# Two tables of steps written anew, and PSUM banks counted on from sequence to sequence

## The reference, cut to what matters

```python
def attention(x):                       # 16 heads of 64, window 64
    xn = x / norm(x) * 16 * gamma
    q, k, v = split(xn @ W_qkv)
    out = softmax(mask(q @ k.T / 8)) @ v          # blocks of 64 queries, this block's and the one before's keys
    out = out * sigmoid(xn @ W_gates + b_gates)   # one gate per token and head
    return out @ W_out

def layer(x, wqkv, wo, w1, w2, ...):    # applied twice; 8 heads of 64, window 128
    h = shift_token(x)                  # the second half of the columns comes from the token before
    q, k, v = split(h @ wqkv)
    q, k = rotary(l2norm(q) * qs, l2norm(k) * ks)
    x = x + softmax(mask(8 * q @ k.T)) @ v @ wo
    a, g = split(layernorm(shift_token(x)) @ w1 + b1)
    return x + (a * gelu(g)) @ w2 + b2

xn = layernorm(x)
result = x + attention(xn) + layer(layer(xn))
```

## Time and profile before

| | us |
|---|---|
| median of three runs | 2006.38 |
| lowest and highest | 2005.78, 2007.42 |
| span of the profiled execution | 2005.4 |
| TensorE busy | 1859.6 |
| ScalarE, VectorE, GpSimd busy | 1383.4, 1289.4, 929.1 |
| DMA: 128.91 MB moved, mean | 64 GB/s |

### The profile page before, as it was taken

One profiled execution on the slowest core, in us unless ns is written; L12 is line 12 of the kernel. 1 busy time (PEld: TensorE's weight loads), 2 busy tenths in 40 slices (PEclk: granted clock), 3 DMA queues, 4 the chain that ended last, 5 costly groups with the idle time before them and its releaser, 6 DMA issues.

```text
span 2005.4 us, 47841 instructions
## 1 busy us (share of the span) xinstructions
PE 1859.6 (93%) x17808; PEld 1564.7 (78%) x17808; DVE 1289.4 (64%) x4125; ACT 1383.4 (69%) x3997; POOL 929.1 (46%) x1315
## 2 busy tenths in 40 slices
PE   6999999999999779999999999999999999999998
PEld 5777787777778658788787887887877878878787
DVE  5543544444443367768777777687777777777765
ACT  5886977778677555866757758667576585675764
POOL 2532542344233454626536446265364562654632
PEclk9999999999999889999999999999999999999999
DMA  3321232223123520110111101304112112011110
GB/s 130 111 81 54 89 90 74 87 71 92 55 88 121 190 67 22 46 54 22 43 34 34 54 14 51 119 15 162 45 32 62 33 46 64 24 53 30 36 46 27
DMA packets 127003, 128.91 MB, mean 64 GB/s; under 512 B 28112, under 2 KB 101940, under 8 KB 126772
## 3 DMA queue, kind: packets, MB, share of 16 engines
q1 hardware_dynamic: 123604, 119.56, 19.2%
q10 hardware_dynamic: 3168, 6.29, 0.9%
HBM read 72.84 MB, written 37.25 MB: 55 GB/s over the span
## 4 chain that ended last, share of the span: by engine, by line
PE 25%; DVE 17%; ACT 16%; POOL 5%; issue 3%; DVEq 0%; POOLq 0%; ACTq 0%; SPq 0%
PE f_bank L1410 11%; ACT f_prob L1644 6%; DVE f_u L1798 5%; POOL f_prob L1363 4%; PE f_scores L1562 3%; DVE f_gu L1794 3%; PE f_bank L1547 3%; ACT f_u L1664 3%; PE f_o_bank L1522 2%; PE f_scores L1489 2%; PE f_bank L1500 2%; ACT f_probT L1585 2%; ACT f_probT L1589 1%; POOL f_norm L1339 1%; ACT f_probT L1588 1%
## 5 line engine op out<-in xcount | busy, mean ns | idle before, releaser
L589 POOL TENSOR_SCALAR a_prob<-a_prob,a_row_inv,a_gate 128x128 f32<-128x128 f32 x512 | 226.1, 459 | 407.0 <-DVE a_row_inv L929 407.0
L1363 POOL TENSOR_SCALAR f_prob<-f_prob,f_row_inv 128x192 f32<-128x192 f32 x512 | 233.4, 476 | 325.8 <-DVE f_row_inv L1740 325.8
L1410 PE MATMUL f_bank<-weights,f_actT 128*128 128x512 f32 x1152 | 307.5, 409 | 9.3 <-DVE f_norm L1688 5.2
L1547 PE MATMUL f_bank<-f_hT,f_w 128*128 128x256 f32 x2112 | 275.4, 285 | 12.5 <-DVE f_gu L1794 12.5
L1547 PEld LDWEIGHTS f_bank<-f_hT,f_w 128*128 128x128 f32 x2112 | 261.1, 190 | 20.0 <-DVE f_gu L1794 18.7
L1410 PEld LDWEIGHTS f_bank<-weights,f_actT 128*128 128x128 f32 x1152 | 208.6, 192 | 66.1 <-DVE f_norm L1688 9.9
L1644 ACT ACTIVATE f_prob<-f_scores,f_neg_max 128x192 f32<-128x192 f32 x512 | 208.5, 426 | 21.3 <-DVE f_neg_max L1732 19.7
L1664 ACT ACTIVATE f_u<-f_gu 128x256 fp32r<-128x256 f32 x192 | 80.2, 418 | 185.4 <-DVE f_gu L1794 185.4
L1339 POOL TENSOR_TENSOR f_norm<-f_norm,f_minus_half 128x16 f32<-128x16 f32 x64 | 192.1, 3003 | 22.7 <-DVE f_norm L1692 19.3
L821 ACT ACTIVATE a_prob<-a_scores,a_neg_max 128x128 f32<-128x128 f32 x512 | 179.9, 390 | 27.8 <-DVE a_neg_max L920 26.5
L612 PE MATMUL a_bank<-a_xT,weights 128*128 128x512 f32 x768 | 193.3, 403 | 1.5 <-DVE a_wgate L898 1.5
(11 more groups left out here) (139 smaller groups left out, 4080.7 us busy)
## 6 DMA issues: line engine op xcount, KB each, us to landing
split_weights<-a_hi_lo SPq DMA_DIRECT2D x16, 512.0 KB, 2.8
x_next<-states SPq DMA_DIRECT2D x32, 256.0 KB, 3.3
tables<-scaled_tables SPq DMA_DIRECT2D x16, 512.0 KB, 5.9
f_x<-states SPq DMA_DIRECT2D x16, 512.0 KB, 5.0
split_weights<-a_hi_lo SPq DMA_DIRECT2D x12, 682.0 KB, 4.1
weights<-split_weights ACTq DMA_DIRECT2D x6, 1024.0 KB, 8.7
f_w<-split_weights SPq DMA_DIRECT2D x4, 1280.0 KB, 11.6
f_v_crossed<-f_v SPq DMA_DIRECT2D x40, 128.0 KB, 2.3
```

Of the source, the lines that this page charges most:

```text
L589: last = nc.gpsimd.tensor_scalar(part, part, row_inv[:, a % 2, head, t:t + 1], gate[:, half, t, h:h + 1], ALU.mult, ALU.mult)
L1363: last = nc.gpsimd.tensor_scalar(part, part, row_inv[:, a % 2, head, t:t + 1], 1.0, ALU.mult, ALU.mult)
L1410: last = nc.tensor.matmul(out, lhs(c, a), rhs(c, b), start=(i == 0), stop=(i == len(order) - 1))
L1547: mm = nc.tensor.matmul(out[:, which * PART:(which + 1) * PART], w1[:, wp, c, col:col + P], hT[:, hp, c, columns_of(a // FH)], start=(i == ...
```

## The change

Both tables of steps are written anew, with the same steps in each. Of the first one a row reads, before and after:

```diff
-A_ORDER = [("load_x", 0), ("scores", 0), ("softmax", 0), ("weights_in", 0), ("scores", 1), ("softmax", 1), ("weigh", 0), ("weights_hi", 0),
+A_ORDER = [("scores", 0), ("scores", 1), ("load_x", 0), ("tables_in", 0), ("softmax", 0), ("softmax", 1), ("project_v", 0),
```

And the banks are numbered through the whole stage: a fill's bank is its number since the start of the stage modulo 3, and it waits for the fill three before it, be that in the pass before. All that named `bank[n % 3]` names `bank_of(it, n)` now, in both stages:

```diff
-def fill_steps(steps, sizes):
+def fills_of(programs, sizes):
-    return [(step, i) for step in steps if step[0] in sizes for i in range(sizes[step[0]])]
+    return [(it, step, i) for it, steps in programs for step in steps if step[0] in sizes for i in range(sizes[step[0]])]
...
-        fills_before, fills_in, fills_last = fill_steps(before, fills), fill_steps(steps, fills), fill_steps(last, fills)
+        all_fills = fills_of([(None, before)] + [(it, steps) for it in range(BATCH - 1)] + [(BATCH - 1, last)], fills)
+        def bank_of(it, n):
+            return bank[(filled.upto(it, n) - 1) % 3]
-        def vacated(it, n):
-            step, i = (fills_before if it is None else fills_last if is_last(it, BATCH) else fills_in)[n]
+        def vacated(fill):
+            it, step, i = all_fills[fill]
...
             def take_bank(it, n):
-                if n >= 3:
-                    pe.wait_ge(*vacated(it, n - 3))
-                elif it is not None:
-                    pe.wait_ge(emptied.sem, emptied.upto(it, -1))
-                    pe.wait_ge(copied.sem, copied.upto(it, -1))
-                return bank[n % 3]
+                fill = filled.upto(it, n) - 1
+                if fill >= 3:
+                    pe.wait_ge(*vacated(fill - 3))
+                return bank_of(it, n)
```

More of the change, by code:

```diff
@@ L791, in gates @@
                     act.wait_ge(bias_negated, 1)
-                nc.scalar.activation(gate_exp[:], bank[n % 3][0:A_HEADS, :], ACT.Exp, bias=bgate[:], scale=-1.0).then_inc(copied.sem, 1)
+                nc.scalar.activation(gate_exp[:], bank_of(it, n)[0:A_HEADS, :], ACT.Exp, bias=bgate[:], scale=-1.0).then_inc(copied.sem, 1)
             for kind, a in before:
@@ L1075, in layers_phase, with bank_of, vacated @@
         copied = count("copied", wholes, credit=1)
-        fills_before, fills_in, fills_last = fill_steps(before, fills), fill_steps(steps, fills), fill_steps(last, fills)
-        def vacated(it, n):
-            step, i = (fills_before if it is None else fills_last if is_last(it, SEQUENCES) else fills_in)[n]
+        all_fills = fills_of([(None, before)] + [(it, steps) for it in range(SEQUENCES - 1)] + [(SEQUENCES - 1, last)], fills)
+        def bank_of(it, n):
+            return bank[(filled.upto(it, n) - 1) % 3]
+        def vacated(fill):
+            it, step, i = all_fills[fill]
             taken = copied if step[0] in wholes else emptied
@@ L1608, in take_raw @@
                     act.wait_ge(filled.sem, filled.upto(it, first + which))
-                    nc.scalar.activation(qk_tok[:, a % TILES, which, :], bank[(first + which) % 3][:], ACT.Copy)
+                    nc.scalar.activation(qk_tok[:, a % TILES, which, :], bank_of(it, first + which)[:], ACT.Copy)
                     if ("project_qk", a - 1) in emptied.firsts(it):
@@ L1614, in take_raw @@
                         act.wait_ge(emptied.sem, emptied.upto(it, -1))
-                    nc.scalar.activation(square[:, which, :], bank[(first + which) % 3][:], ACT.Square).then_inc(raw_taken.sem, 1)
+                    nc.scalar.activation(square[:, which, :], bank_of(it, first + which)[:], ACT.Square).then_inc(raw_taken.sem, 1)
             for kind, a in before:
@@ L1793, in iteration @@
                         place = PART if j == FH - 1 else 0
-                        nc.vector.scalar_tensor_tensor(out=gu[0:m, a % 2, :], in0=bank[n % 3][0:m, place:place + PART], scalar=b1_cols[0:m, 0, j:j + 1],
+                        nc.vector.scalar_tensor_tensor(out=gu[0:m, a % 2, :], in0=bank_of(it, n)[0:m, place:place + PART], scalar=b1_cols[0:m, 0, j:j + 1],
                                                        in1=gu[0:m, a % 2, :], op0=ALU.add, op1=ALU.mult).then_inc(emptied.sem, 1)
```

111 lines of the change are left out of this document (56 added, 55 removed).

## The result

The changed kernel takes 1963.6 us (1962.2 to 1964.2, 4 runs) beside 2006.9 for the kernel before: 0.978 of it, 95% interval 0.977 to 0.980. That is 43 us faster where I forecast 11, and outside the range of 1982 to 2012.

What follows compares the result with a forecast made beforehand. TensorE's work plus its holes, 145.8 us in all, was taken to bound the kernel. First stage -14, passage +9.5, second stage -7, late projection loads +0.5 gave -11, so 1995.5 us; range 1982 to 2012.

Steps and rivals of the forecast that it cites:

- The passage, +9.5: Between the stages: SyncE's later store of the row constants delays TensorE's second stage by 9.5 us, bounds +5 and +15.
- The other estimate of the prediction: Passage between the stages: with 2 us for each of two landings, the loss is +5 us instead of +9.5.
- The banks, 0: Start of a first-stage pass: counting the banks on gives nothing by itself, since two score steps cover the wait.
- First stage, -3.7 a pass: First stage: filled TensorE holes save 3.7 us in three passes and 2.7 in the last, 14 us together.
- My bound of 24 for the first stage: First stage: upper bound of the gain, 24 us, with all holes shown gone, 6.0 a pass.
- Second stage, -0.45 a half: Second stage: holes in transposes 4 and 7 close, 0.45 us a half, 7 us over sixteen; bounds 21 gained, 10 lost.
- Rope 3 behind transpose_h 1 pushes VectorE's chain: Second stage, up steps: the later rope 3 pushes VectorE's chain by some 0.6 us, so no gain of 0.78 counted.
- rival 3: Second stage: later rope 3 and bias on GpSimd block VectorE's up products, 0.6 us a half slower, 2012.5 us; 20%.
- The other meeting that the prediction names: First stage: rms_apply's products no longer meet GpSimd's table scaling, saving VectorE about two microseconds that TensorE did not await.
- Filled holes come back at the ups: Second stage: each filled hole returns at the up steps, as the chain of VectorE and ScalarE has no slack.
- Rival 1: Only the first stage gains; holes filled in the second come back at the up steps: 2002.5 us; 22%.
- Rival 2: Nearly all holes close, up steps included, and the passage costs only its lower bound: 1980 us; 13%.

Runs made afterwards that it cites:

- a4: The changed kernel with weights_out 6, rows_in and rows_out put back to SyncE's places before the change: 1948.3 us, ratio 0.971; run again 1950.3, 0.973.
- c4: The changed kernel with only rows_in and rows_out put back early, weights_out 6 still ahead of the first rows: 1956.7 us, ratio 0.974 to the kernel before.
- a3: The kernel before with both old tables, only the banks counted on as in the change: 2005.8 us, ratio 1.000.
- b1: The kernel before with project_qk 16 between transposes 14 and 15 and weights_hi, lo and out 6 late: 1997.2 us, ratio 0.996.
- c3: The kernel before with rope 3 and, right behind it, x1_bias moved behind transpose_h 1: 2004.7 us, ratio 0.999.
- b3: The kernel before with rope 3 alone moved behind transpose_h 1, x1_bias left where it was: 2029.6 us, ratio 1.013.
- b2: The kernel before with down 3 moved behind up 4 and down 4 behind up 7: 2005.7 us, ratio 1.001.
- d1: The kernel of a4 with transpose 1 behind scores 3 and down 7 ahead of transpose_qk 2: 1946.6 us, ratio 0.971 to the kernel before.
- c2: The kernel before with the second stage's order from up 0 to the end of a half as in the change: 1998.0 us, ratio 0.995.
- a2: The kernel before with the change's second-stage table and banks, the first stage's table old: 1977.1 us, ratio 0.985.
- a1: The kernel before with the change's first-stage table and banks, the second stage's table old: 1988.0 us, ratio 0.991.
- c1: The kernel before with transpose_qk 0 and take_o 1 behind values 3, rope 2 behind take_o 3: 1999.7 us, ratio 0.996.

## Why the prediction was wrong

The sign was right, and so were most of the places; the sum was not. Of the 32 us by which it fell short, some 11 are in the first stage (20 in the three full passes and 5 in the last, against 13.8), 2 in the passage (7.4 instead of 9.5), some 16 in the second stage (23.1 in fifteen halves and 0.6 in the last, less 0.7 ahead of them, against 6.8), and 3.4 are the clock of the kernel before in its last pass. Point by point:

- *The passage, +9.5.* The chain was right (shown by a4), and the bounds +5 and +15 held; the hole grew by 7.4. From the issue of weights_out 6 to TensorE's start the prediction has 15.5 us (677.5 to 693.0) and the profile 13.5 (649.37 to 662.91): the ten issues took 0.6 more than forecast, the constants 3.8 us from the end of the last load's issue (655.84) to their store instead of 2.5, and from the store's issue to TensorE it was 3.2 instead of 7.2, since the store landed in 2.6 us instead of 6. That the last pass with the passage lost 8.9, so near to 9.5, is luck: it holds the 1.3 of the wait at transpose 1. The other estimate of the prediction, 2 us for each landing and so +5, was off by about as much the other way.
- *SyncE's order inside the first stage, no term.* The late rows_in and rows_out make SyncE late for keep_keys at the start of the next pass, and that cost 0.8 to 1.3 us in each pass but the first (after against a4 and c4).
- *The banks, 0.* Right: a3.
- *First stage, -3.7 a pass.* The mechanism was right and the size wrong. Between profiles of the old table and the new one (a3 and a4, the mean of three passes) a pass lost 7.1 us of waits, start to start. The single terms: transpose 0, 0.51 (forecast 0.55); values 4, 0.96 (0.87); project_out 1, 0.60 (0.43); transpose 6, 0.48 (0.31); values 10, 0.55 (0.48); transpose 5, +0.37 (+0.5). All near. But some 0.5 of the 7.1 is the clock, which fell in two of a3's three passes and in one of a4's: where it stayed full, a pass takes 163.1 and 156.4, 6.7 less. And transposes 14 and 15 gave 2.6 (forecast 0.6 + 0.98), where b1, the moves that I had named, gives 2.05, and what gives the rest is not run; transposes 2 and 3 gave 0.5 where I counted nothing; and some ten waits of 0.1 to 0.3 us that leave no idle row (transposes 8 and 9, scores 11, project_out 10, project_v 7 among them) gave some 0.7 us.
- *The step that failed: a hole costs what its idle row says, and where there is no idle row there is no delay.* I added up idle rows. The window of the third pass shows 3.9 us less idle and 5.8 us less time, and over the kernel 16.7 us went out of TensorE's busy time. My bound of 24 for the first stage, "all holes shown", was thus no bound: the three full passes gave 20 (493.1 to 473.0), and the last one 6.3 without the late stores (154.9 in a3, 148.6 in a4), 26 together.
- *Second stage, -0.45 a half.* Mis-sized by the most. In the medians, a half is 2.1 us shorter in a4 than in a3: 1.4 in the middle of the half (forecast 0.56 + 0.1), 0.7 in the ups and downs (forecast 0, less 0.2 for the late transpose_qk 3), and at the start 0.1 is lost (forecast 0). Of the middle, project_qk 3 gave 0.37 instead of 0.1, and transposes 4 and 7 0.40 and 0.48 instead of 0.22 and 0.34.
- *Rope 3 behind transpose_h 1 pushes VectorE's chain.* Wrong: c3 shows no loss. What the text of rival 3 feared, GpSimd's bias beside VectorE, is real, but it needs the bias at another place (b3). The other meeting that the prediction names went as it said: the products of rms_apply, 32 in all, took 22.4 us before and 13.3 after, 2.3 less a pass.

```profile
L883 DVE SCALAR_TENSOR_TENSOR x_next<-a_x_tok,a_rms,a_gamma_row 128x256 f32<-128x256 f32 x32 | 22.4, 761 | 10.9 <-POOL a_rms L559 6.1 <-PE a_bank L694 4.6 <-DVE a_x_tok L866 0.2
```

```profile
L886 DVE SCALAR_TENSOR_TENSOR x_next<-a_x_tok,a_rms,a_gamma_row 128x256 f32<-128x256 f32 x32 | 13.3, 476 | 12.2 <-POOL a_rms L564 12.1 <-DVE a_x_tok L869 0.2
```

- *Filled holes come back at the ups.* Right for one or two moved downs (b2, d1), wrong for the whole new order (c2), which moves VectorE's and GpSimd's work with TensorE's; that this is the reason is argued, not shown. Rival 1, which stood on this, falls by a2.
- *Rival 2, nearly all holes close,* named 1980 with 13%. Its direction was the right one. It, too, summed idle rows.

Shown are the parts of the table (a1, a2), the passage (a4, c4), the end of the pass (b1) and the order of the ups (c2). The two stages' savings, 19 and 30, add to 5 us more than the change itself. In the profiles the change's fifteen halves are 2.8 us longer than a2's, with the clock down for 43 us instead of 33, and its first stage up to the second stage's first matmul is 2.4 longer than a1's, and these make the 5; the cause of either stays open. Beside c1 and c2, 12 of the second table's 30 us remain. Some 8 are the wait of transpose_qk 1, 0.53 in fifteen halves, which c1 has and the whole table has not, and 3.4 may be the clock of the kernel before in its last pass; what of the table spares transpose_qk 1 stays open.

## What to carry to other kernels

An idle row ahead of a pipelined matmul understates its delay: add what a row outlasts its place (its length less the distance from start to start in an undisturbed run), and look for steps that start late without an idle row, by their distances from start to start. When steps are moved in one table for all engines, ask of each move what the other queues then do in another order: a bias that changed places on GpSimd cost 24 us, and seven loads with the store behind them at the end of SyncE's queue 5, and 3 more in waits at the start of the passes, where SyncE was late for other steps. Look behind a new hole, too: in b3 a wait of 2.1 us a half took the clock down, for another 1.3. A hole filled by one moved step is often only handed on; judge a new order by the sum of all waits for the same product.

## What the runs showed of the hardware

- A matmul of 256 columns in a run begins 0.12 us behind the one ahead, and its row is 0.285 long (the earlier trace rows and the working beside it).
- Two VectorE operations of ln_apply took 3.07 us beside a GpSimd addition of 2.35 us, and 516 ns each without it.
- TensorE's clock fell for 3.4 us at a time at the start of halves of the changed kernel, after a stretch in which TensorE was busy 4.22 of 6.00 us; DMA was busy 0.99 in the stretch of lower clock. In b3 it fell behind the wait at transpose_h 1, after 3.66 busy of 6.00 us, with DMA's share at 0.00 in the stretch of lower clock: a burst of DMA beside it is not needed.
- The store of the row constants, 390 KB from SyncE, landed 2.6 us after its issue in the change's passage, and 5.9 and 6.6 in c4 and a4, right behind the tables' load of 512 KB. The earlier trace rows has 3.9 and 9.9; just ahead of the 9.9, three loads of 1024 KB had been issued.
